# A graph-attention kernel on one core: five row buffers, 64 gathers in the projection block, x loaded inside the attention stage

## The chip, the cores and the metric

The kernel runs on one core of one Trainium2 chip, as one program that does two layers of a graph network with their feed-forward parts. The metric is the device time of one execution in microseconds (us). Engines are named as in the profile: PE (TensorE), DVE (VectorE), ACT (ScalarE), POOL (GpSimd) and SP (SyncE); "POOLq" or "SPq" is an engine's queue of DMA issues.

## The reference, cut to what matters

There are 6250 nodes with 256 features and 100000 edges, sorted by their target `dst`. The first layer is attention over the edges with 8 heads of 32, the second a mean over the same edges. Each is followed by experts.

```python
# layer 0, on x normed by row: W_fc, W_e, attn_* and bias are weights
ft = (feat @ W_fc).reshape(N, H, D)
eh, et = einsum('nhd,hd->nh', ft, attn_h), einsum('nhd,hd->nh', ft, attn_t)
ee = einsum('ehd,hd->eh', (edge_attr @ W_e).reshape(-1, H, D), attn_e)
e = leaky_relu(eh[src] + ee + et[dst])
a = exp(e - segment_max(e, dst)[dst]) / segment_sum(exp(...), dst)[dst]
x = x + segment_sum(ft[src] * a[:, :, None], dst) + bias
x = x + shared(norm(x)) + top-2-of-4 experts(norm(x))
# layer 1: mean over incoming edges of (norm(x) @ W_src)[src], plus the features; batch norm; relu
x = x + that
x = x + expert(argmax(router(norm(x))))(norm(x))       # 32 experts
```

## The kernel before

The 100000 edges are cut into 784 tiles of 128 edges (`ES = 784`), and attend works on chunks of 16 tiles (`UT = 16`), 49 of them (`NCH`). A tile's source rows (256 features and 8 score parts, `RW` = 264 values) are fetched by one indirect DMA on POOL, one index for each of the 128 partitions: `indirect_dma_start(..., SRCT[:, t:t + 1])`. The stages follow each other, each an `nc.Block()` whose end is a barrier of all engines:

- `front` (the projection block) loads x, norms it, multiplies by W_fc and stores the rows `ft_rows` to memory. Beside this it loads `edge_attr` in 49 "edge chunks": SP loads one (L406, L407) when ACT is through with the one before (`attr_T1`), PE transposes it, ACT copies it out (L622), PE multiplies (L531), ACT keeps the result in V (L628). POOL scatters `et` to the edges' starts (L501, 50 indirect DMAs) and then gathers the first two attention chunks, `GF = 2`, 32 tiles (L509). DVE scans F (L835), adds V and F in two halves (L840), and SP stores the halves as `score_parts` (L486).
- `attend` has two blocks. The first (L905 to L950) sets constants: POOL's selection masks and an iota, DVE's memsets and MSEL, which is made of the iota. The second runs the chunks. POOL gathers the rows of chunk c into row buffer c % GS, with `GS = 4`: buffers 0 to 2 lie in `GX`, buffer 3 has its own tile. From chunk 4 on it waits ahead of each four tiles (`WB = 4`) for `g_free`, which PE raises (L1143, L1144) after having waited for its own product of the four tiles. POOL clears the accumulator ACC (L977) after the gathers of chunks 2 and 3, and ACT waits for that before its first instruction. For each chunk SP loads PRE (L1006), DVE makes scores (L1160), running maxima (U_f, L1181), sums and shares in a chain with PE and ACT, multiplies the rows by their weights, four tiles at a time (L1278), and builds the one-hot matrices AHOT (three buffers, L1172); PE multiplies rows by one-hots, tile by tile (L1138), into four PSUM banks, and ACT adds them up in ACC (L1066). The chain of chunk c + 1 is interleaved by hand with the weights of chunk c, in the body `rest`; `first` does chunk 0's chain. The loop is fully written out. When all gathers are out, POOL clears FFN tiles, and SP then loads the FFN weights (L1013).
- `rank_rows` turns ACC and stores it by rows, 49 stores of 128 KB, with 7 row buffers (L1516). In the first layer ("a") SP's queue holds ahead of these the load of the bias and of x (6.4 MB, into `GX`, L1505 and L1508). In the second layer ("b") it has a weight to multiply by and no such loads.
- `gated_experts` uses x and bias. `sum_segments` sums the second layer's rows: 784 gathers (L1376), groups of 8 tiles, 4 groups of buffers, two sets of four PSUM banks; PE waits for each bank (`pfree`) at every second tile. `rank_rows` b, the mean layer and the routed experts follow.

All instructions of an engine run in program order, and DMAs of SP's queue are issued in order.

## Time and profile before

| | |
|---|---|
| median of 3 runs | 4067.09 us (4066.4 to 4073.57) |
| the profiled execution, its own time | 4042.07 us |
| its span in the trace | 4040.4 us |
| mean granted TensorE clock | 0.705 of 2.4 GHz |
| busy over the span | PE 61%, PEld 53%, DVE 50%, POOL 45%, ACT 32% |
| instructions | 51661 |

The stages in the profiled execution, by the starts of their first instructions in the trace: projection block 0 to 485.6 us, attend to 1760.8, rank_rows a to 1825.6, gated experts and norm to about 2340, sum_segments to about 3479, rank_rows b to about 3526, and the rest to 4040.4. The rows further down are read with start and duration in us, then engine, line, operation, output and inputs; the bracket at a row's end is how long the engine had been idle and what released it. "remote" is an event without a recorded sender, "issue" is time in which the engine waited for nothing that the profile shows.

### The profile page before, as it was taken

What the parts mean: (1) busy time and instruction counts of PE and PEld (TensorE: products, weight loads), DVE (VectorE), ACT (ScalarE), POOL (GpSimd) and SP (SyncE); (2) the same over time, 40 slices, a digit from 0 to 9 for tenths busy, and PEclk for the clock granted to TensorE, in tenths of its full rate; (3) what the DMA queues carried; (4) which work ended last, traced back from release to release, by engine and by line L of the source; (5) the groups of instructions that cost most, each with busy time, mean ns of one, the idle gap of its engine ahead of it and who ended that gap; (6) DMA issues with size and microseconds to landing.
All of it is one profiled execution on the core that took longest, in us unless ns stands there. A gap on an engine that the chain in (4) does not pass through costs nothing. (4 is left out here: it accounts for less than half of the span.)

```text
span 4040.4 us, 51661 instructions
## 1 busy us (share of the span) xinstructions
PE 2474.9 (61%) x12916; PEld 2128.5 (53%) x12916; DVE 2006.0 (50%) x6407; ACT 1290.8 (32%) x4654; POOL 1799.1 (45%) x1888
## 2 busy tenths in 40 slices
PE   6964636666666666655899944545545445646348
PEld 5853525555555555544677634544444444535347
DVE  7930247777777777745645432322323223354325
ACT  2311123334334344442233222323323223352113
POOL 0043156666666666403100066666666666241255
PEclk9966666667766776767888856666666666756579
DMA  6343323333333333345000033333333333330043
GB/s 182 100 102 85 120 70 91 91 91 90 89 89 91 91 91 90 76 116 164 20 21 21 18 90 92 90 93 90 93 93 90 93 90 92 103 94 1 25 127 94
DMA packets 262938, 348.49 MB, mean 86 GB/s; under 512 B 153465, under 2 KB 193519, under 8 KB 261143
## 3 DMA queue, kind: packets, MB, share of 16 engines
q0 software_dynamic: 87936, 235.05, 20.8%
q1 hardware_dynamic: 174726, 110.32, 10.7%
q8 instruction: 105, 1.72, 0.2%
q14 instruction: 171, 1.40, 0.1%
HBM read 288.25 MB, written 61.20 MB: 86 GB/s over the span
## 5 line engine op out<-in xcount | busy, mean ns | idle before, releaser
L1376 POOL DMA_INDIRECT Gb<-normed_rows,SRCT x784 | 743.3, 948 | 741.4 <-SPq L1368 358.7
L1396 PE MATMUL pAb<-HOTb,Gb 128*128 128x128 f32 x3136 | 580.5, 336 | 564.0 <-issue 551.2
L1396 PEld LDWEIGHTS pAb<-HOTb,Gb 128*128 128x128 f32 x3136 | 524.2, 247 | 620.6 <-issue 603.5
L1438 DVE TENSOR_TENSOR ACC<-ACC,pAb 128x256 f32 x784 | 330.7, 422 | 800.1 <-DMA sums_by_rank<-rrowa 576.4
L981 POOL DMA_INDIRECT GX<-ft_rows,SRCT x560 | 532.2, 950 | 355.5 <-PEq L1144 211.7
L1138 PE MATMUL apA<-AHOT,GX 128*128 128x129 f32 x2368 | 481.8, 385 | 220.0 <-DVE GX L1278 195.6
L1138 PEld LDWEIGHTS apA<-AHOT,GX 128*128 128x128 f32 x2368 | 449.9, 292 | 255.7 <-DVE GX L1278 223.6
L1066 ACT ACTIVATE ACC<-apA 128x254 f32 x784 | 301.0, 384 | 694.6 <-PE apA L1138 299.1
L1415 ACT ACTIVATE HOTb<-OFFb 128x1024 f32<-128x1024 f32 x98 | 103.6, 1057 | 769.8 <-DMA sums_by_rank<-rrowa 757.5
L1411 ACT ACTIVATE OFFb<-iota,NRELb 128x128 f32<-128x128 f32 x784 | 239.8, 388 | 6.7
L981 POOL DMA_INDIRECT G<-ft_rows,SRCT x192 | 183.2, 954 | 111.0 <-PEq L1144 62.2
L1138 PE MATMUL apA<-AHOT,G 128*128 128x129 f32 x768 | 156.2, 385 | 69.3 <-DVE G L1278 62.9
L1138 PEld LDWEIGHTS apA<-AHOT,G 128*128 128x128 f32 x768 | 145.9, 291 | 80.6 <-DVE G L1278 74.2
L531 PE MATMUL pS<-VB,eT 128*128 128x16 f32 x784 | 117.9, 294 | 109.3 <-issue 60.2
L531 PEld LDWEIGHTS pS<-VB,eT 128*128 128x128 f32 x784 | 113.7, 231 | 124.7 <-issue 62.4
L1278 DVE TENSOR_TENSOR GX<-GX,apV 128x1024 f32<-128x1024 f32 x148 | 176.4, 1193 | 0.4 <-PE apV L1118 0.4
L1605 POOL DMA_INDIRECT Y<-sums_by_rank,RANKI x50 | 48.4, 968 | 241.3 <-POOLq L150 143.0
L1181 DVE TENSOR_TENSOR_SCAN U_f<-PENU,pU 128x128 f32<-128x128 f32 x49 | 20.6, 421 | 243.6 <-remote 194.0
L1067 ACT ACTIVATE FL<-apA 128x4 f32<-128x4 f32 x784 | 134.4, 171 | 0.0
L622 ACT ACTIVATE eT<-pE 128x512 f32<-128x512 f32 x98 | 55.7, 607 | 198.4 <-remote 101.4
L1172 DVE TENSOR_TENSOR AHOT<-apL,RELT 128x1024 f32<-128x1024 f32 x98 | 118.7, 1212 | 0.0
L2180 POOL DMA_INDIRECT rows_by_expert<-PAY,POSI x50 | 49.7, 995 | 150.8 <-DVE POSI L2319 135.9
(386 smaller groups left out, 4615.9 us busy)
## 6 DMA issues: line engine op xcount, KB each, us to landing
ebuf<-in_edge_attr_dram SPq DMA_DIRECT2D x49, 448.0 KB
Gb<-normed_rows,SRCT POOLq DMA_INDIRECT x784
rows_by_expert<-ffn_PADT SPq DMA_DIRECT2D x1, 10360.0 KB
sT<-rows_by_expert SPq DMA_DIRECT2D x80, 129.5 KB
GX<-ft_rows,SRCT POOLq DMA_INDIRECT x592
sums_by_rank<-rrowa SPq DMA_DIRECT2D x49, 128.0 KB, 1.7
sums_by_rank<-rrowb SPq DMA_DIRECT2D x49, 128.0 KB, 1.7
GX<-in_x_dram SPq DMA_DIRECT2D x11, 560.0 KB
```

The costliest lines, as they stand in the source:

```text
L531: last = nc.tensor.matmul(pS[:, m * 2 * H0:(m + 1) * 2 * H0], eT[c % 2][:, m * EP:(m + 1) * EP], VB[:, :], start=True, stop=True)
L981: pool.indirect_dma_start(G[c % GS][:, m, :], None, FT[:, :], bass.IndirectOffsetOnAxis(ap=SRCT[:, t:t + 1], axis=0)).then_inc(g_in[c % GS ...
L1066: nc.scalar.activation(acc[:, :, ds(r + 1, EP - 1)], sums[:, :, 1:EP], ACT.Copy)
L1067: nc.scalar.activation(FL[:, :, f:n + 1:n - f], sums[:, :, 0:HW:EP], ACT.Copy).then_inc(pfree[b], 1)
L1138: last = nc.tensor.matmul(pA[b][:, f * HW:(f + 1) * HW], G[c % GS][:, m, f * 128:(f + 1) * 128], HOT[k][:, m, :], start=True, stop=True)
L1172: nc.vector.tensor_tensor(HOT[k][:, h * HT:(h + 1) * HT, 0:EP], pL[0:EP, 256:256 + EP].unsqueeze(1).to_broadcast([EP, HT, EP]), RELT[:, ds ...
L1278: nc.vector.tensor_tensor(v, v, pV[0:EP, 0:128].rearrange("p (h m) -> p h m", m=UT)[:, :, m:m + WB].rearrange("p h m -> p m h").unsqueeze( ...
L1376: pool.indirect_dma_start(G[g % R][m][:, :], None, TABLE[:, :], bass.IndirectOffsetOnAxis(ap=SRCT[:, t:t + 1], axis=0)).then_inc(g_in[g % ...
L1396: last = nc.tensor.matmul(pA[b][:, o:o + EP], G[k][m][:, c * 128:(c + 1) * 128], HOT[k % 2][:, m, :], start=True, stop=True)
L1411: nc.scalar.activation(OFF[k2][:, m, :], iota[0:EP, 0:EP], ACT.Abs, bias=NREL[k2][:, m:m + 1])
L1415: nc.scalar.activation(HOT[k2][:, :, :], OFF[k2][:, :, :], ACT.Relu, bias=1.0, scale=-1.0).then_inc(hot[k2], 1)
L1438: last = nc.vector.tensor_tensor(acc[:, :, ds(b, EP)], acc[:, :, ds(b, EP)], pA[q][:, o:o + KD * EP].rearrange("p (c r) -> p c r", c=KD), ...
```

## The change

1. `GS` goes from 4 to 5 and `GF` from 2 to 4. The fourth buffer (`G3`) is made before `front`, which now gathers four chunks (64 tiles) at L509's place. To make room, front's scratch tiles share memory, with no additional waits, and AHOT has two buffers instead of three.
2. The add of V and F and the stores of `score_parts` go in seven parts instead of two; part h waits for the first 7 (h + 1) edge chunks instead of all 49.
3. attend's set-up block is merged into the main block. ACT's first instruction waits for DVE's memsets, and ACT waits for ACC at the loading of the first chunk's row numbers, ahead of its first write. POOL clears ACC ahead of its first gather there (chunk 4's), and the FFN tiles between the gathers of chunks 4 and 5. POOL waits for PE's product of the bank directly, and PE does not wait for its own.
4. SP loads bias and x at the end of attend's queue, each part of x behind PE's last product of the chunk whose rows lay there: chunk 45 for the first two parts, 46 and 47 for the others.
5. In `sum_segments` PE waits once in a group of 8 tiles for the last bank of the set, and DVE signals once.

```diff
 SL = 3
-GS = 4
-GF = 2
+GS = 5
+GF = 4
 XPARTS = ((0, 5), (5, 15), (15, 30), (30, NT))
...
+def arow(GX, GE, k, m):
+
+    to, o = (GX, k) if k < SL else (GE, k - SL)
+    return to[:, (o * UT + m) * (D + H0):(o * UT + m + 1) * (D + H0)]
 
...
                     load(c)
                 pv = PRED.rearrange("(p j) h -> p (j h)", j=ES)
-                for h in range(2):
+                for h in range(NPT):
                     a = slice(h * HF * H0, (h + 1) * HF * H0)
                     sp.wait_ge(parts_ready, h + 1)
                     sp.dma_start(pv[:, a], V[:, a]).then_inc(parts_out, 16)
-                sp.wait_ge(parts_out, 32)
+                sp.wait_ge(parts_out, 16 * NPT)
...
                     nc.vector.tensor_tensor_scan(head(h), CONT[:, :], head(h), C0[:, h:h + 1], ALU.mult, ALU.add)
                 dve.drain()
-                dve.wait_ge(v_ready, NCH)
-                for h in range(2):
+                for h in range(NPT):
+                    dve.wait_ge(v_ready, (h + 1) * (NCH // NPT))
                     a = slice(h * HF * H0, (h + 1) * HF * H0)
                     nc.vector.tensor_tensor(V[:, a], V[:, a], F[:, a], ALU.add).then_inc(parts_ready, 1)
...
                     c, m = divmod(t, UT)
+                    if t == GF * UT:
+                        nc.gpsimd.memset(ACC[:, :], 0.0).then_inc(acc_zero, 1)
                     if t == GS * UT:
-                        nc.gpsimd.memset(ACC[:, :], 0.0).then_inc(acc_zero, 1)
...
                     if m % WB == 0 and c >= GS:
 
-                        pool.wait_ge(g_free, c * WG + m // WB + 1)
+                        pool.wait_ge(prod[NBK - 1], (c - GS) * CPB + m // NBK + 1)
                     pool.indirect_dma_start(G[c % GS][:, m, :], None, FT[:, :],
                                             bass.IndirectOffsetOnAxis(ap=SRCT[:, t:t + 1], axis=0)
...
+                xv = x.rearrange("(p i) d -> p (i d)", i=NT)
+                sp.dma_start(BI[:, :], bias.rearrange("h d -> (h d)").partition_broadcast(P)).then_inc(bi_in, 16)
+                for n, (i0, i1) in enumerate(XPARTS):
+
+                    used = max(c for c in range(NCH) if c % GS < SL and c % GS * UT * RW < i1 * D)
+                    sp.wait_ge(prod[NBK - 1], (used + 1) * CPB)
+                    for one in PARTS:
+                        sp.dma_start(X[one, i0 * D:i1 * D], xv[one, i0 * D:i1 * D]).then_inc(xm_in[n], 16)
...
+                    if c == 0:
+                        act.wait_ge(acc_zero, 1)
...
                 act.load(regs[1], BASEI[0:1, 0:HT])
-                act.wait_ge(acc_zero, 1)
+                act.wait_ge(set_ready, 1)
                 unrolled(NCH, SL, first, rest)
                 finish(1, NCH + 1)
...
-                pe.sem_inc(g_free, GS * WG)
-                pe.sem_inc(hot_free, SL)
+                pe.sem_inc(hot_free, 2)
...
                             last = nc.tensor.matmul(pA[b][:, f * HW:(f + 1) * HW], G[c % GS][:, m, f * 128:(f + 1) * 128],
-                                                    HOT[k][:, m, :], start=True, stop=True)
+                                                    HOT[c % 2][:, m, :], start=True, stop=True)
                         last.then_inc(prod[b], 1)
-                        if m % WB == WB - 1:
-
-                            pe.wait_ge(prod[b], c * CPB + m // NBK + 1)
-                            pe.sem_inc(g_free, 1)
                     pe.sem_inc(hot_free, 1)
                     if more:
                         own_shares(c + 1)
...
+                dve.drain()
+                dve.sem_inc(set_ready, 1)
+                nc.vector.tensor_copy(pL[0:EP, 256:256 + EP], iota[0:EP, 0:EP])
...
+                dve.wait_ge(sel2, 1)
+                for h in range(H0):
+                    nc.vector.scalar_tensor_tensor(MSEL[:, :], BU[:, :], float(h * UT), MSEL[:, :], ALU.is_equal, ALU.add)
+                    dve.drain()
+                nc.vector.tensor_copy(pL[:, 400:400 + UT], MSEL[:, :])
+                dve.drain()
...
                         dve.wait_ge(hot_free, c + 1)
-                        nc.vector.tensor_copy(HOT[k][:, :, EP], GOES[:, ds(c * UT, UT)])
-                    nc.vector.tensor_tensor(HOT[k][:, h * HT:(h + 1) * HT, 0:EP],
+                        nc.vector.tensor_copy(HOT[c % 2][:, :, EP], GOES[:, ds(c * UT, UT)])
+                    nc.vector.tensor_tensor(HOT[c % 2][:, h * HT:(h + 1) * HT, 0:EP],
...
                 def group(r, g, k):
                     pe.wait_ge(hot[k % 2], r * 2 + k // 2 + 1)
+
+                    if g >= 2:
+                        pe.wait_ge(pfree[last_bank(k)], r * 2 + k // 2)
                     for m in range(K):
 
                         pe.wait_ge(g_in[k][m], r * 16 + 16)
                         b = bank(k, m)
-                        if m % 2 == 0:
-                            pe.wait_ge(pfree[b], r * 2 + k // 2 + 1)
                         for c in range(KD):
                             o = m % 2 * KD * EP + c * EP
...
-                        if m % 2:
+                        if m == K - 1:
                             last.then_inc(pfree[q], 1)
                         dve.drain()
 
```

On POOL, from the end of front's scatters to the first waits of the loop in the kernel before. GX and G are row buffers, SRCT the indices, arows_free PE's signal, aprod3 the product semaphore of the fourth bank:

```order
L501 DMA et_at_starts<-ETS,FIRSTI 100352x8 x49
L509 DMA GX<-ft_rows,SRCT 128x264 [waits src_ready,row_stored1,row_stored0]
L509 DMA GX<-ft_rows,SRCT 128x264 x31
...
L906 UNCONDITIONAL_BRANCH [waits barrier_Pool_Activation_PE_DVE_SP_gather]
...
L927 IOTA BU 128x16 [waits sel_set]
...
L972 UNCONDITIONAL_BRANCH [waits barrier_Pool_Activation_PE_DVE_SP_gather]
L981 DMA GX<-ft_rows,SRCT 128x264 x16
L981 DMA G<-ft_rows,SRCT 128x264 x16
L977 MEMSET ACC 128x12760
L981 DMA GX<-ft_rows,SRCT 128x264 [waits arows_free]
L981 DMA GX<-ft_rows,SRCT 128x264 x3
```

The same place on POOL in the changed kernel, whose line numbers differ:

```order
L504 DMA et_at_starts<-ETS,FIRSTI 100352x8 x49
L512 DMA GX<-ft_rows,SRCT 128x264 [waits src_ready,row_stored1,row_stored0]
L512 DMA GX<-ft_rows,SRCT 128x264 x47
L512 DMA G<-ft_rows,SRCT 128x264 x16
...
L930 UNCONDITIONAL_BRANCH [waits barrier_Pool_Activation_PE_DVE_SP_gather]
...
L951 IOTA BU 128x16 [waits sel_set]
L957 MEMSET ACC 128x12760
L975 DMA G<-ft_rows,SRCT 128x264 x16
L960 MEMSET ffn_E 128x512
...
L970 AFFINE_SELECT ffn_SEL<-ffn_SEL 4x256 [waits ffn_w_pad]
L975 DMA GX<-ft_rows,SRCT 128x264 [waits aprod3]
L975 DMA GX<-ft_rows,SRCT 128x264 x3
```

The memset of ACC now stands ahead of attend's first gathers, of which 16 are left there instead of 32, and the waits are for the product.

On PE, the second group of four tiles in chunk 0's body and what follows it, in the kernel before (aweighted is DVE's weight multiply, ends_ready its step ahead of the joint maxima):

```order
L1138 MATMUL apA<-AHOT,GX 128x129 [waits aprod3,abank_free0,aweighted]
L1138 MATMUL apA<-AHOT,GX 128x129
...
L1138 MATMUL apA<-AHOT,GX 128x129 [waits abank_free3]
L1138 MATMUL apA<-AHOT,GX 128x129
L1099 MATMUL apQ<-Qends,HSEL 8x112 [waits aprod3,ends_ready]
L1138 MATMUL apA<-AHOT,GX 128x129 [waits abank_free0,aweighted]
```

The same on PE in the changed kernel:

```order
L1130 MATMUL apA<-AHOT,GX 128x129 [waits abank_free0,aweighted]
L1130 MATMUL apA<-AHOT,GX 128x129
...
L1130 MATMUL apA<-AHOT,GX 128x129 [waits abank_free3]
L1130 MATMUL apA<-AHOT,GX 128x129
L1089 MATMUL apQ<-Qends,HSEL 8x112 [waits ends_ready]
L1130 MATMUL apA<-AHOT,GX 128x129 [waits abank_free0,aweighted]
```

The wait for aprod3, PE's own product, is gone ahead of each group and ahead of L1099's step.

On SP, the end of attend's queue and the start of rank_rows', in the kernel before:

```order
L1013 DMA ffn_E<-in_L_ffn_eW_dram 128x64 x4
L971 UNCONDITIONAL_BRANCH [waits ffn_w_in]
L1501 UNCONDITIONAL_BRANCH [waits barrier_Pool_Activation_PE_DVE_SP_release]
L1505 DMA ffn_BI<-in_L_gnn_bias_dram 125x256
L1508 DMA GX<-in_x_dram 112x1280
L1508 DMA GX<-in_x_dram 13x1280
...
L1508 DMA GX<-in_x_dram 112x5120
L1508 DMA GX<-in_x_dram 13x5120
...
L1516 DMA sums_by_rank<-rrowa 128x256
```

The same on SP in the changed kernel:

```order
L993 DMA ffn_E<-in_L_ffn_eW_dram 128x64 x4
L996 DMA ffn_BI<-in_L_gnn_bias_dram 125x256
L1002 DMA GX<-in_x_dram 112x1280 [waits aprod3]
L1002 DMA GX<-in_x_dram 13x1280
...
L1002 DMA GX<-in_x_dram 112x5120 [waits aprod3]
L1002 DMA GX<-in_x_dram 13x5120
L929 UNCONDITIONAL_BRANCH [waits ffn_w_in]
L1506 UNCONDITIONAL_BRANCH [waits barrier_Pool_Activation_PE_DVE_SP_release]
...
L1515 DMA sums_by_rank<-rrowa 128x256
```

The eight loads of x and the bias now stand ahead of the barrier, with waits for PE, and the stores of rank_rows have nothing ahead of them.

## Rows read from the trace of the kernel before

**Rows 1.** Windows: length, busy us of PE, PEld, DVE, ACT, POOL; clock, DMA share.
```profile
311.00:351.00 40.00, 6.96 (x28) 6.19 (x28) 0.00 (x0) 1.36 (x3) 30.30 (x32) 0.54 0.44 118
486.00:557.00 71.00, 1.74 (x6) 0.90 (x6) 14.11 (x66) 2.93 (x7) 43.14 (x41) 0.50 0.29 65
1770.00:1790.00 20.00, 0.00 (x0) 0.00 (x0) 0.00 (x0) 0.31 (x1) 0.00 (x0) 0.59 1.04 231
```

**Rows 2.** L509 as a source line, then POOL's timeline behind it.
```profile
L509 POOL DMA_INDIRECT GX<-ft_rows,SRCT x32: 945/949/999, 310.9 to 349.8; - x32
...
485.62 0.11 POOL L909 MEMSET HSEL<- 128x8 f32 x1 [134.87 <-ACTq L905]
```

**Rows 3.** ACT's timeline beside and behind the gathers: the edge chunks.
```profile
325.64 0.60 ACT L622 ACTIVATE eT<-pE 128x512 f32<-128x512 f32 x1 [10.54 <-remote]
...
362.19 1.09 ACT L622 ACTIVATE eT<-pE 128x512 f32<-128x512 f32 x2 [35.78 <-remote]
...
369.15 0.60 ACT L622 ACTIVATE eT<-pE 128x512 f32<-128x512 f32 x1 [5.70 <-PE pE L522]
```

**Rows 4.** Timeline, end of front and start of attend, DVE and SP.
```profile
472.42 6.76 DVE L840 TENSOR_TENSOR V<-V,F 128x3136 f32<-128x3136 f32 x2 [17.07 <-ACT V L628]
...
488.59 1.68 DVE L945 SCALAR_TENSOR_TENSOR MSEL<-BU,MSEL 128x16 f32<-128x16 f32 x7 [2.49 <-POOL BU L927]
...
491.72 2.73 SPq L1006 DMA_DIRECT2D PRE<-score_parts  x3
...
494.96 0.37 DVE L1160 TENSOR_TENSOR SCT<-GX,PRE 128x128 f32<-128x128 f32 x1 [3.57 <-DMA PRE<-score_parts]
```

**Rows 5.** Timeline, attend's first chain: POOL, ACT and DVE.
```profile
532.14 10.75 POOL L977 MEMSET ACC<- 128x12760 f32 x1
543.02 0.31 ACT L1023 ACTIVATE CTU<-CONTU 128x129 f32<-128x129 bf16 x1 [70.63 <-POOL ACC L977]
...
543.73 0.42 DVE L1181 TENSOR_TENSOR_SCAN U_f<-PENU,pU 128x128 f32<-128x128 f32 x1 [47.99 <-ACT PENU L1024]
...
557.43 1.22 DVE L1278 TENSOR_TENSOR GX<-GX,apV 128x1024 f32<-128x1024 f32 x1
...
560.67 0.38 ACT L1066 ACTIVATE ACC<-apA 128x254 f32 x1 [7.97 <-PE apA L1138]
```

**Rows 6.** Timeline inside the attention loop: POOL and DVE.
```profile
1006.82 0.95 POOL L981 DMA_INDIRECT GX<-ft_rows,SRCT  x1 [0.30 <-issue]
1009.35 0.42 DVE L1181 TENSOR_TENSOR_SCAN U_f<-PENU,pU 128x128 f32<-128x128 f32 x1 [4.28 <-remote]
...
1009.92 0.95 POOL L981 DMA_INDIRECT GX<-ft_rows,SRCT  x1 [2.15 <-PEq L1144]
...
1016.37 0.95 POOL L981 DMA_INDIRECT GX<-ft_rows,SRCT  x1 [1.75 <-PEq L1144]
```

**Rows 7.** Waits from 900 to 1300 us: us in total, times, longest.
```profile
DVE U_f L1181 <- remote: 70.9, 16, 5.3
```

**Rows 8.** DVE's timeline in the last two chunks, without gathers.
```profile
1700.97 0.37 DVE L1160 TENSOR_TENSOR SCT<-G,PRE 128x128 f32<-128x128 f32 x1
...
1703.22 0.42 DVE L1181 TENSOR_TENSOR_SCAN U_f<-PENU,pU 128x128 f32<-128x128 f32 x1 [0.34 <-PE pU L1093]
...
1721.39 0.37 DVE L1160 TENSOR_TENSOR SCT<-GX,PRE 128x128 f32<-128x128 f32 x1
```

**Rows 9.** Timeline of rank_rows a, then SP's stores in rank_rows b.
```profile
1761.12 4.58 SPq L1508 DMA_DIRECT2D GX<-in_x_dram  x8
...
1766.60 56.73 SPq L1516 DMA_DIRECT2D sums_by_rank<-rrowa  x49
...
1796.04 2.49 DVE L1499 COPY rrowa<-pRTa 128x256 f32<-128x256 f32 x7 [27.67 <-DMA sums_by_rank<-rrowa]
...
3482.65 42.74 SPq L1516 DMA_DIRECT2D sums_by_rank<-rrowb  x49
```

**Rows 10.** POOL's timeline in sum_segments, first gather behind a pause.
```profile
2918.01 0.95 POOL L1376 DMA_INDIRECT Gb<-normed_rows,SRCT  x1 [3.26 <-DMA sums_by_rank<-rrowa]
```

More of the change, by code:

```diff
@@ L312, in front @@
         SD = sb(s, "SDa", [P, NT])
[L313 to L314 removed]
         row = [sb(s, f"row{k}", [P, GT, D + H0]) for k in range(2)]
         ETS = sb(s, "ETS", [128, NT * H0])
+        DEG = sb(s, "DEG", [P, NT])
         V = sb(s, "V", [EP, ES * H0])
@@ L843, in attend @@
 def attend(nc, sb, ps, sem, sems, pace, FT, PRED, CONTU, WHOLE, GX, g_in, ident, iota, SRCT, RELT, GOES, BASEI, ACC,
-           FFN, weights):
+           FFN, weights, GE, more):
     NCH = ES // UT
@@ L1120, in first @@
                 def first(c, k, i):
-                    for step in (scores, ends, own_shares, attention, shares_before):
+                    scores(c)
+                    pe.wait_ge(sel2, 1)
+                    for step in (ends, own_shares, attention, shares_before):
                         step(c)
@@ L1421, in _ @@
             def _(dve):
-                for m in range(K):
-                    dve.sem_inc(pfree[m], 1)
                 nc.vector.memset(ACC[:, :], 0.0)
@@ L1444, in _, with rank_rows @@
                 groups(dve, group)
-def rank_rows(nc, sb, ps, sem, sems, pace, tag, ident, weight, ACC, RSUMD, x=None, X=None, xm_in=None, bias=None, BI=None,
-              bi_in=None):
+def rank_rows(nc, sb, ps, sem, sems, pace, tag, ident, weight, ACC, RSUMD):
     K = 7
```

142 lines of the change are left out of this document (63 added, 79 removed).

## The prediction

> **What bounds the kernel now.** I read the busy times by stage first, then the timelines of POOL, ACT, DVE and SP where stages meet, and last the waits inside the attention loop. "B" is the start of attend's first block, 485.6 us here.
>
> Two stretches stand out. From 311 to 351 us DVE does nothing and PE 7 us of 40, while POOL issues 32 gathers; from 486 to 557 us PE is busy for 1.7 us of 71 [rows 1]. In the first, L509's 32 gathers start from 310.9 to 349.8, one every 1.254 us, and end at 350.7 [rows 2]. What the other engines have to do there is the edge chunks (ACT L622 and its like), and ACT gets one of them at 325.64 and the next at 362.19, 11.4 us after POOL's last gather's end; the next comes 7.0 us later [rows 3]. So while POOL issues indirect DMAs, the edge chunks crawl, and that queue, not POOL, sets the end of the projection block: POOL is idle for 134.87 us behind its gathers [rows 2]. I can't name the resource. The row only says "remote".
>
> In the second stretch POOL sets everything: two blocks' set-up, 32 gathers, then the 10.75 us memset of ACC, and behind it ACT's first instruction, which had waited 70.63 us. DVE's U_f waited 47.99 us for it, and the first weight multiply (L1278) starts at 557.43, 71.8 us after B [rows 5].
>
> In the loop a 16-tile chunk takes 25.0 us (16 waits of U_f in 400 us), of which 4.4 us are U_f waiting for "remote" [rows 7]. DVE alone needs 20.4 us: that is the step between two scores (L1160) at the end, where no gather is left to issue and U_f waits 0.34 us [rows 8]. The wait ends 1.6 us after the end of the last gather that POOL could issue (1007.77 to 1009.35), and POOL goes on only 0.6 us later [rows 6]. So the loop is a ring: POOL's burst of eight gathers, release of the others, PE's next four tiles, POOL again.
>
> **The change part by part**, against the profiled execution's 4042.07 us.
>
> (1) 32 more gathers in front: 32 x 1.254 = 40.1 us more stream, 351 to 391 us. In the 36.6 us between ACT's rows at 325.64 and 362.19 one edge chunk got through, so one more will in 40 us. Without the stream a chunk costs 7.0 us at most [rows 3], and I count 4. So I take +36. The bounds are 0 (the chunks run beside the stream) and +40.
>
> The Trainium skill, "DMA: Bandwidth & Descriptors", section "Issuing engines are not separate DMA queues", says that DMAs of all issuing engines run on the same 16 DMA engines and interleave. By that rule the edge loads would share, not stop, and this term would be 0. The rows at 325.64 and 362.19 speak against it, since there the loads' users stand still while the stretch's DMA share is 0.44 [rows 1, 3]; rival A below is this case.
>
> (2) score_parts in seven parts: now the last V is there at 472.4, the two adds behind it take 6.76 us, and the block ends 6.4 us after them [rows 2, 4]. Afterwards only the last seventh is added behind the last chunk, 6.76 / 7 = 1.0 us. That is -5.8; I take -5.5, since the number of stores grows from two to seven, though all but the last lie under the edge chunks.
>
> (3) attend's start. Afterwards no gather and no second barrier stands ahead of the first chain. SP's PRE load needs 3.2 us from issue to scores (491.72 to 494.96, [rows 4]); DVE's eight MSEL steps wait for POOL's iota until B + 3.0 and take 0.24 us each [rows 4], so PRE is there first and scores come near B + 5.3. From scores to U_f is 2 us (1700.97 to 1703.22, with a weight between, [rows 8]), and from U_f to the first weight 13.7 us (543.73 to 557.43, [rows 5]). So the first weight is at B + 21 instead of B + 71.8: -51. The ACC memset runs from B + 2.9 to B + 13.7, under the chain; its first reader's write comes 3.2 us after the first weight (560.67), at B + 24, so it has 10 us to spare and costs nothing, and without that cover it would cost up to 10.75.
>
> (4) Chunk 4's 16 gathers now stand at B + 13.7 to B + 33.8, that is beside chunk 0 and the start of chunk 1, where before POOL had nothing to issue in the first chain. By the ring's rule U_f of chunk 1, due near B + 23, is let go at B + 35.4: +12. In the loop the same wait is 4.4. Bounds 0 and +15; I take +10.
>
> (5) In the loop, POOL waits for PE's product semaphore itself, and PE no longer waits for its own product four times a chunk. POOL's pause is 2.15 us at the burst's end [rows 6] of which the hand-over is a small part, and PE's scores and BU transposes no longer queue behind a completion. I take 0.15 us a chunk, 48 x 0.15 = -7; bounds 0 and -20. A fifth buffer moves which chunk a gather is for, not when its four tiles are done: the release is the product of the current chunk either way. AHOT with two buffers instead of three: DVE writes the one-hots of chunk c + 1 while PE works on c, and the buffer it takes was chunk c - 1's. The wait is met, 0.
>
> (6) The last gathers go out one chunk earlier, so one more chunk has no 4.4 us wait: -4.4. The FFN memsets go ahead of chunk 5's gathers and under the same DVE chain: 0. They are six small steps, once, next to ACC's 10.75 us.
>
> (7) x. Now SP issues the eight x loads at 1761.12, ahead of rank_rows' stores, which share its queue. DVE has copied seven rows and then waits 27.67 us for a store to leave, until 1796.04; all 49 stores take 56.7 us [rows 9]. Without the loads there is no such wait. From 1796.04 on, the 42 stores left need 27.3 us, 0.65 us each; 49 such are 32, and they start some 4 us sooner, without SP's 4.58 us of load issues. So 56.7 + 4 - 32 = 29 less; I take -27. The upper side is 42.7 us for 49 stores, as in rank_rows b [rows 9], which would make it -18; with nothing for the earlier start it is -14. The loads themselves (6.4 MB) now wait for the products of chunks 45 to 47. Ahead of them in SP's queue stand only the PRE and FFN loads, behind them nothing that attend needs, and the last chunks have no other DMA: 0, unless DVE suffers from them (rival D).
>
> (8) sum_segments: PE's waits on banks go from four in a group of eight tiles to one, and DVE's signals too. POOL pauses 3.26 us behind every 16 gathers and everybody starts again with it [rows 10]; that law has no bank in it. 0; bounds +5 and -147 (the pause, 3 us x 49, gone).
>
> Sum: 36 - 5.5 - 51 + 10 - 7 - 4.4 - 27 = **-49**: 3993 us for an execution like the profiled one. The median of the runs is 4067.09, 25 us more, spread over the same work; I keep the difference and not the ratio: 4067 - 49 = **4018 us**.
>
> **Rivals.**
> A. The edge chunks run beside the longer stream. For it: an idle DMA share of over half. Against: rows 3. Then (1) is 0: 4018 - 36 = 3982.
> B. The ring opens, because PE's self-wait was what tied POOL's burst to the others, and sum_segments' law too. For it: the waits end with PE's, every time. Against: POOL, not PE, ends first. 45 chunks x 4.4 = -198, and up to -147 more: 3820 and below.
> C. Slower. PE signals sooner, so the next four tiles are done before POOL's burst of eight ends, and it becomes one of twelve; U_f is then let go four gathers later, 4 x 1.254 = 5.0 us a chunk. For it: POOL needs only 20.1 us of the 25 for its 16 gathers, and it now has a buffer more. Against: the releases inside a chunk are 6.45 us apart (1009.92 to 1016.37, [rows 6]), longer than four gathers take. In all 45 chunks it is +226: 4244; it decides from 49 / 5.0, that is from 10 chunks of 45, and wherever it holds in 12 or more the kernel is slower.
> D. The x loads hold up the last chunks as they held up the stores. Against: what waited there was a store in the same queue. 6.4 MB at the 231 GB/s of that stretch [rows 1] are 27 us of transfer, which would take back all of (7): 4018 + 27 = 4045, still faster.
> E. The change does not do what it says, in that the first chain is held until chunk 4's gathers are out (B + 35.4 plus what is left of the chain, some 15 us): (3) shrinks to -22 and (4) goes: 4037.
>
> **How the numbers follow.** Forecast 0.48; A 0.16; B in full or part 0.10; C 0.11; D 0.09; E 0.06. A difference under 0.2% (8 us) can't be told from no change here, so "same" is 4059 to 4075. The forecast's own bounds: for the fast side (1) part hidden and (5) -20, for the slow side (4) +15 and (7) -14: 3985 to 4040. A, D and E are in 3960 to 4060. The range 3945 to 4072 leaves out B's full form and C: 0.18. Faster: 0.44 of the forecast, all of A and B, 0.05 of D, 0.03 of E: 0.78. Same: 0.04 of the forecast, 0.02 each of C, D and E: 0.10. Slower: 0.09 of C, 0.02 of D, 0.01 of E: 0.12.
>
> **What would show it.** (1) ACT's first edge chunk behind the stream near 402 us instead of 362, the block's end near 516; if near 480, A. (2) One add of 1 us behind the last V. (3) First weight 21 us after the block's start. (4) U_f of chunk 1 with a wait of 10 us or so. (5) U_f still waits some 4 us a chunk on "remote" and POOL still pauses; if these are gone, B; if bursts are twelve long, C. (7) 49 stores in 32 to 43 us and no wait of DVE over 1 us. I am wrong most easily in (1), (4) and the loop, where an unnamed resource is priced by its pattern.

## The result, and the profile after

| | before | changed |
|---|---|---|
| median, 4 runs each | 4070.33 us (4066.4 to 4082.15) | 4009.84 us (4003.71 to 4013.74) |
| ratio | | 0.9843, 95% interval 0.9825 to 0.9862 |
| the profiled execution's span | 4040.4 us | 4012.0 us |

The change takes 60.5 us off, 1.6%; the forecast was 49 off the 4067 known then, at 4018. Measured again on two chips, called chip 1 and chip 14 here, with the kernel before beside it, it gave 0.9855 (0.9838 to 0.9872) and 0.9839 (0.9810 to 0.9867). The two traces differ by 28.4 us only. The profiled execution of before lies 28 us under this median (25 under the 4067), that of the changed kernel 4 us over its own, so terms that are read from this pair of traces do not add up to the measured difference.

Stage by stage in the two traces, with the gap to before that has piled up by then:

| reached | before, us | changed, us | gap |
|---|---|---|---|
| end of the projection block | 485.6 | 521.9 | +36.3 |
| first weight multiply | 557.4 | 545.6 | -11.8 |
| scores of the last chunk | 1721.4 | 1718.6 | -2.8 |
| end of rank_rows a | 1825.6 | 1793.6 | -31.9 |
| end of rank_rows b | 3527.7 | 3494.1 | -33.5 |
| end | 4040.4 | 4012.0 | -28.4 |

Busy times by stage of the changed kernel (window, length, busy us of PE, PEld, DVE, ACT, POOL; clock, DMA share, GB/s), the answer to [rows 1]:

```profile
311.00:351.00 40.00, 6.83 (x28) 6.17 (x28) 0.00 (x0) 1.36 (x3) 30.30 (x32) 0.54 0.44 118
351.00:391.00 40.00, 0.00 (x0) 0.00 (x0) 0.00 (x0) 0.00 (x0) 30.34 (x32) 0.50 0.41 108
486.00:557.00 71.00, 39.84 (x177) 33.28 (x175) 45.07 (x101) 10.37 (x25) 29.78 (x32) 0.57 0.34 90
1770.00:1790.00 20.00, 13.96 (x47) 6.55 (x46) 12.36 (x30) 7.12 (x18) 0.00 (x0) 0.51 0.58 203
```

The first row is as before. The second is the 40 us more of POOL's stream: nobody else does anything. From 486 to 557 PE now works 40 us instead of 1.7, and from 1770 to 1790 the engines work where all stood still.

The gathers of L512 (L509 before) as source lines, with duration in ns and the first and last start:

```profile
L512 POOL DMA_INDIRECT GX<-ft_rows,SRCT x48: 945/949/999, 310.9 to 369.9; - x48
L512 POOL DMA_INDIRECT G<-ft_rows,SRCT x16: 945/949/954, 371.1 to 389.9; - x16
```

ACT's timeline in the changed kernel, beside and behind this stream, the answer to [rows 3]:

```profile
326.07 0.60 ACT L625 ACTIVATE eT<-pE 128x512 f32<-128x512 f32 x1 [10.54 <-issue]
...
393.33 0.60 ACT L625 ACTIVATE eT<-pE 128x512 f32<-128x512 f32 x1 [66.50 <-remote]
402.37 0.60 ACT L625 ACTIVATE eT<-pE 128x512 f32<-128x512 f32 x1 [8.44 <-remote]
402.87 0.27 ACT L631 ACTIVATE V<-pS 128x128 f32<-128x128 f32 x1
```

The same chunk's last row in the kernel before:

```profile
363.16 0.28 ACT L628 ACTIVATE V<-pS 128x128 f32<-128x128 f32 x1
```

An edge chunk is copied in two halves; the row at 362.19 in the kernel before had both, here they come at 393.33 and 402.37. The V row behind them is 39.7 us later (402.87 instead of 363.16), which is 32 gathers. None got through in the longer stream. In both kernels the chunk comes some 11.5 us after the stream's end, not at once.

The timeline from the end of the projection block to chunk 2's scores, the answer to [rows 4, 5]. L843 is the add, L986 the PRE load, L957 ACC's memset, L1167 the scores, L1285 the weight multiply, L1188 U_f:

```profile
517.19 1.09 DVE L843 TENSOR_TENSOR V<-V,F 128x896 f32<-128x896 f32 x1 [10.59 <-ACT V L631]
...
521.95 6.34 SPq L986 DMA_DIRECT2D PRE<-score_parts  x4
...
524.71 10.73 POOL L957 MEMSET ACC<- 128x12760 f32 x1
...
527.50 0.38 DVE L1167 TENSOR_TENSOR SCT<-GX,PRE 128x128 f32<-128x128 f32 x1
```

```profile
530.56 4.92 DVE L1178 COPY AHOT<-GOES 128x16 f32<-128x16 f32 x1
530.62 4.86 DVE L1179 TENSOR_TENSOR AHOT<-apL,RELT 128x1024 f32<-128x1024 f32 x1
531.75 3.73 DVE L1201 TENSOR_TENSOR_SCAN U_fs<-CTU,U_ex 128x128 f32<-128x128 f32 x1
...
535.59 0.23 DVE L1208 TENSOR_SCALAR Qends<-apL,U_f 128x16 f32<-128x16 f32 x1
...
544.89 0.37 DVE L1167 TENSOR_TENSOR SCT<-GX,PRE 128x128 f32<-128x128 f32 x1
...
545.58 1.21 DVE L1285 TENSOR_TENSOR GX<-GX,apV 128x1024 f32<-128x1024 f32 x1
547.76 0.42 DVE L1188 TENSOR_TENSOR_SCAN U_f<-PENU,pU 128x128 f32<-128x128 f32 x1 [0.96 <-PE pU L1083]
...
574.44 0.37 DVE L1167 TENSOR_TENSOR SCT<-GX,PRE 128x128 f32<-128x128 f32 x1
```

Behind the last V one add of 1.09 us is left, and the next stage begins 4.7 us after the add's start, where it was 13.2. Scores come 5.6 us after the block's start and the first weight 23.7. In between stand DVE rows that are new: the copy of L1178 takes 4.92 us (0.15 before), and the rows that start behind it, the one-hots' L1179 and the scan L1201, 4.86 and 3.73 (1.22 and 0.41 before). All three end at 535.48, when POOL's memset of ACC ends (524.71 + 10.73 = 535.44), and the next step follows at once. From L1179's start to L1208's it is 5.0 us where before's trace has 1.9, so the chain loses 3.0 us.

The loop, one burst's end and the release of U_f (answer to [rows 6]), and rank_rows a (answer to [rows 9]), in the changed kernel's timeline:

```profile
1007.50 0.95 POOL L975 DMA_INDIRECT GX<-ft_rows,SRCT  x1 [0.30 <-issue]
1010.23 0.42 DVE L1188 TENSOR_TENSOR_SCAN U_f<-PENU,pU 128x128 f32<-128x128 f32 x1 [3.48 <-remote]
...
1010.88 0.95 POOL L975 DMA_INDIRECT G<-ft_rows,SRCT  x1 [2.44 <-PE apA L1130]
```

```profile
1760.16 31.25 SPq L1515 DMA_DIRECT2D sums_by_rank<-rrowa  x49
1793.64 0.39 SPq L1613 DMA_DIRECT2D rows_by_expert<-ffn_PADT  x1
```

U_f is let go 1.8 us after the end of the last gather of a burst of eight, and POOL goes on 0.65 us later: the ring is as it was. The 49 stores take 31.3 us instead of 56.7.

### The profile page after: what moved, and what is told of

The parts are those of the page before. It is cut to its first block and busy times, and to the rows that moved or that the text cites. A ratio compares the mean times of both kernels' runs of the same rounds, so it can differ in the third digit from the quotient of the medians.

```text
span 4012.0 us, 51163 instructions
## 1 busy us (share of the span) xinstructions
PE 2464.4 (61%) x12916; PEld 2133.0 (53%) x12916; DVE 2006.2 (50%) x6412; ACT 1289.1 (32%) x4654; POOL 1800.5 (45%) x1888
## 5 line engine op out<-in xcount | busy, mean ns | idle before, releaser
L975 POOL DMA_INDIRECT GX<-ft_rows,SRCT x432 | 412.0, 954 | 262.9 <-PE apA L1130 127.5
L1130 PE MATMUL apA<-AHOT,GX 128*128 128x129 f32 x1920 | 396.0, 391 | 171.1 <-DVE GX L1285 146.7
L1130 PEld LDWEIGHTS apA<-AHOT,GX 128*128 128x128 f32 x1920 | 373.0, 298 | 197.0 <-DVE GX L1285 167.2
L975 POOL DMA_INDIRECT G<-ft_rows,SRCT x288 | 274.5, 953 | 172.9 <-PE apA L1130 88.2
L1130 PE MATMUL apA<-AHOT,G 128*128 128x129 f32 x1216 | 244.7, 384 | 101.0 <-DVE G L1285 85.5
L1130 PEld LDWEIGHTS apA<-AHOT,G 128*128 128x128 f32 x1216 | 230.7, 291 | 116.8 <-DVE G L1285 96.5
L1285 DVE TENSOR_TENSOR GX<-GX,apV 128x1024 f32<-128x1024 f32 x120 | 143.1, 1193 | 0.0
L1179 DVE TENSOR_TENSOR AHOT<-apL,RELT 128x1024 f32<-128x1024 f32 x98 | 122.4, 1249 | 0.0
L2379 POOL DMA_INDIRECT out_dram<-sO,sID x80 | 77.8, 973 | 77.7 <-issue 40.9
```

The lines of the kernel that those rows point to most:

```text
L975: pool.indirect_dma_start(G[c % GS][:, m, :], None, FT[:, :], bass.IndirectOffsetOnAxis(ap=SRCT[:, t:t + 1], axis=0)).then_inc(g_in[c % GS ...
L1130: last = nc.tensor.matmul(pA[b][:, f * HW:(f + 1) * HW], G[c % GS][:, m, f * 128:(f + 1) * 128], HOT[c % 2][:, m, :], start=True, stop=True)
L1179: nc.vector.tensor_tensor(HOT[c % 2][:, h * HT:(h + 1) * HT, 0:EP], pL[0:EP, 256:256 + EP].unsqueeze(1).to_broadcast([EP, HT, EP]), RELT[: ...
L1285: nc.vector.tensor_tensor(v, v, pV[0:EP, 0:128].rearrange("p (h m) -> p h m", m=UT)[:, :, m:m + WB].rearrange("p h m -> p m h").unsqueeze( ...
```

## The experiments

Each kernel is the changed one with a short edit. The theory to be tested was the prediction's, called S: a stream of POOL's indirect DMAs starves the other engines, wherever it stands. "To starve" means here that they start next to no instructions. The first four kernels and the kernel before beside them ran on one chip, chip 15.

**Where the gathers stand.** The edit is `GF = 2`.

> The changed kernel with GF = 2: 32 gathers in the projection block instead of 64, and 48 instead of 16 ahead of the first wait in attend (60 us of issue instead of 20). Theory S (a stream of indirect DMAs holds up the other engines wherever it stands): the projection block ends near 482 us instead of 522, and chunks 0 to 3 of attend take about 40 us more, so the total stays within 10 us of the changed kernel's, ratio to before 0.984 give or take 0.002. Rival (the stream costs only in the projection block, since attend's first chain has its rows already and runs beside it): 36 to 40 us less than the changed kernel, ratio near 0.975.

Measured: 4025.53 us, ratio 0.9866 (0.9838 to 0.9895). That is 0.002 above the changed kernel's 0.9843, just outside the 0.002 that were allowed, but its interval covers them. Its timeline, POOL at the block's end and DVE's scores of chunks 1 and 2:

```profile
483.81 0.10 POOL L933 MEMSET HSEL<- 128x8 f32 x1 [131.94 <-POOLq L151]
```

```profile
506.79 0.37 DVE L1167 TENSOR_TENSOR SCT<-GX,PRE 128x128 f32<-128x128 f32 x1
...
583.37 0.37 DVE L1167 TENSOR_TENSOR SCT<-GX,PRE 128x128 f32<-128x128 f32 x1
```

The projection block ends 38.1 us sooner (35 against two kernels on the same chip whose block is the changed kernel's, 518.9 and 519.5), and the step from chunk 1's scores to chunk 2's takes 76.6 us instead of 29.6, 47 more. It is no wait for chunk 2's rows: POOL's 16 gathers for it are out at 517.2. So the 32 gathers cost some 40 us in front or beside the chain, and a little more in attend. The rival, that they cost only in front, falls.

**Cutting the stream in front.** POOL waits for one more edge chunk ahead of every fifth DMA:

```diff
                 for i in range(NT):
+                    if i >= 10 and (i - 10) % 5 == 0:
+                        pool.wait_ge(v_ready, 28 + (i - 10) // 5)
...
                 for t in range(GF * UT):
+                    i = NT + t
+                    if (i - 10) % 5 == 0:
+                        pool.wait_ge(v_ready, min(28 + (i - 10) // 5, NCH))
```

> The changed kernel with POOL's stream in the projection block cut: from its tenth indirect DMA on (50 scatters, then 64 gathers), POOL waits ahead of every fifth for one more edge chunk to be through. Nothing is left out. Theory S with a threshold (the others are held up only once a stream is long, some 10 DMAs or more): edge chunks come every 6 to 8 us from 260 us on, the last V is there near 430 us instead of 517, POOL's last gather near 430 instead of 391, and the block ends 60 to 90 us sooner; total near 3930, ratio near 0.965. Rival N (no threshold: edge chunks and POOL's issue exclude each other at any length): each group of five costs its 6.3 us plus 1.6 us plus a chunk's 5 us, so the 21 chunks end no sooner than now and the block ends at 520 to 560; ratio 0.984 to 0.994.

Measured: 3930.06 us, ratio 0.9636 (0.9607 to 0.9665). It was repeated beside the changed kernel, on chip 14:

> Groups of five indirect DMAs per edge chunk in the projection block, otherwise the changed kernel. On a chip where a chunk takes 25 us: the block ends 80 to 90 us sooner than in the changed kernel of the same call, total 80 us less, ratio 0.964 as before. On a chip where it takes 20: the groups cost 0 to 20 us, since POOL would have finished at 390 and the edge chunks at 400, ratio 0.976 to 0.981.

> The changed kernel beside the kernel before and beside the kernel with groups of five. On a chip where an attention chunk takes 25 us: ratio 0.984 to 0.986 as twice so far, projection block's end near 522 us. On a chip where it takes 20: no starving, the 32 more gathers are hidden, ratio near 0.976, block's end near 404.

Measured: 3902.19 us with groups of five, ratio 0.9633 (0.9607 to 0.9658), and 3988.58 for the changed kernel, 0.9839: 86 us between the two on one chip. POOL's timeline with groups of five on chip 15, at three groups of scatters and at the end of the block:

```profile
270.71 0.97 POOL L506 DMA_INDIRECT et_at_starts<-ETS,FIRSTI  x1 [4.04 <-ACT V L636]
...
277.72 0.97 POOL L506 DMA_INDIRECT et_at_starts<-ETS,FIRSTI  x1 [0.94 <-issue]
...
289.35 0.97 POOL L506 DMA_INDIRECT et_at_starts<-ETS,FIRSTI  x1 [5.55 <-ACT V L636]
```

```profile
434.70 0.10 POOL L938 MEMSET HSEL<- 128x8 f32 x1 [6.29 <-POOLq L151]
```

POOL waits 4.04 us and 5.55 between groups for "ACT V", that is for an edge chunk (0.94 in a third case, put down to "issue"), and idles 6.29 us at the end instead of 131. The block ends at 434.7 us instead of 521.9 (519 on this chip). So the same 114 DMAs and the same 21 edge chunks fit beside each other in this version, and a rule without a threshold (rival N), by which they exclude each other at any length, falls. This version beats both kernels.

But the waits did not cut the whole stream. From 375 to 418.8 us the edge chunks were ahead of them and POOL issued 30 gathers with no pause. Here is what the engines did meanwhile: a window, and rows of DVE, POOL and ACT:

```profile
375.00:390.00 15.00, 14.81 (x60) 12.86 (x60) 13.82 (x8) 2.73 (x6) 12.52 (x9) 0.51 0.65 178
```

```profile
376.18 14.05 DVE L843 TENSOR_TENSOR_SCAN F<-xnT,C,F 128x784 f32<-128x784 f32 x8 [47.43 <-DMA F<-et_at_starts]
380.83 1.44 POOL L517 DMA_INDIRECT GX<-ft_rows,SRCT  x1 [0.30 <-issue]
422.19 1.08 ACT L630 ACTIVATE eT<-pE 128x512 f32<-128x512 f32 x2 [16.23 <-remote]
```

Beside DVE's scans a gather takes 1.44 us instead of 0.95, so that one goes out every 1.74 us and not every 1.25, and PE is busy for 14.8 us of 15, with edge chunks 5 to 7 us apart. Some 9 us after the gathers are back at 1.25 us apart (from 396.5) ACT stops for 16.2 us. The trace from chip 14 has the same: ACT goes on through the gathers of 1.44 us and stops for 8.4 us some 8 us after the full rate is back. So it is not the length alone that starves, but a length at the full rate, and part of this version's gain may come from the slower gathers.

**Longer bursts in the loop.** One wait per chunk:

```diff
-                    if m % WB == 0 and c >= GS:
-                        pool.wait_ge(prod[NBK - 1], (c - GS) * CPB + m // NBK + 1)
+                    if m == 0 and c >= GS:
+                        pool.wait_ge(prod[NBK - 1], (c - GS + 1) * CPB)
```

> The changed kernel with one wait of POOL per chunk in attend, for all 16 tiles of the chunk five before, instead of four waits for four tiles each: bursts of 16 gathers. Theory S: the others are held until the burst is out, U_f's wait goes from 4 us to 8 or more per chunk, a chunk from 25 us to 29 or more, total 150 us or more above the changed kernel, ratio 1.02 or more. Rival P (the pauses at the four waits are what costs, one pause of 3 us takes the place of 2.2 + 1.8 + 1.8): a chunk takes 23 us as 16 gathers do in sum_segments, total 80 to 90 us below the changed kernel, ratio near 0.963.

Measured: 4275.98 us, ratio 1.0484 (1.0455 to 1.0514). DVE's scores of two chunks and POOL's first gather of a burst:

```profile
1004.53 0.37 DVE L1167 TENSOR_TENSOR SCT<-GX,PRE 128x128 f32<-128x128 f32 x1
...
1035.44 0.37 DVE L1167 TENSOR_TENSOR SCT<-GX,PRE 128x128 f32<-128x128 f32 x1
```

```profile
1033.45 0.99 POOL L975 DMA_INDIRECT GX<-ft_rows,SRCT  x1 [11.41 <-PE apA L1130]
```

A chunk takes 30.9 us: some 20 of issue, then POOL idle for 11.4 until PE's last product. The others catch up only in the pause. S said 29 or more, and rival P (23 us) falls. S had also named U_f as the place, and there it was wrong: U_f's wait is 0.3 us or less on average, and DVE waits at the next step, for the exponentials.

**x in the rows' queue.** The loads of bias and x go back to the head of rank_rows.

> The changed kernel with the loads of bias and x back at the head of rank_rows' queue. If the x term stands as the two traces read it (104.2 us from the last scores to the end of rank_rows before, 75.1 after), the total rises by 29 us over the changed kernel, ratio near 0.991. Rival (the loads only moved their cost into the last chunks, and the 29 us come from the end of attend): under 10 us, ratio near 0.985.

Measured: 4041.75 us, ratio 0.9916 (0.9886 to 0.9946), 0.007 above the changed kernel. SP's timeline of it:

```profile
1753.13 4.57 SPq L1505 DMA_DIRECT2D GX<-in_x_dram  x8
1758.60 56.41 SPq L1513 DMA_DIRECT2D sums_by_rank<-rrowa  x49
```

The stores take 56.4 us again, and from the last chunk's scores to the end of rank_rows it takes 101.7 us, where the changed kernel takes 75.1. So the loads cost nothing in the last chunks: the x term stands.

**Four kernels that ran on chip 9.** There the kernel before took 3580.96 us (3574.04 to 3587.09).

> The changed kernel with the projection block's indirect DMAs in groups of ten per edge chunk. Theory S with a threshold of some 10: each group of ten lets one or two edge chunks through, POOL's last gather comes near 410 us, and 11 edge chunks are left for then: the block ends near 470 to 480, total 3965. With a threshold well under ten: as the changed kernel without groups, 10 chunks x 5.3 behind 104 x 1.254 + 10 x 7 us of groups, block end at 500 to 520, total 4000 or more.

> The changed kernel with the projection block's indirect DMAs in groups of three per edge chunk instead of the five of an earlier run, and attend's memset of ACC in eight pieces. Theory S: the edge chunks run at their own 5 to 7 us, the last V comes at 385 to 400 us instead of 427, but 21 chunks let only 63 DMAs through, so 41 gathers follow behind them and POOL ends 51 us later, at 440 to 455; the block ends some 15 us later than with groups of five. Pieces of ACC: if DVE's 4.9 us copy at the start of attend (now 530.6 to 535.5, ending with POOL's memset) is held by that one memset, it takes 1.5 us at most, and the first weight multiply comes 20 us after the block's start instead of 23.7; if not, it stays at 23.7. Total near 3940.

> The changed kernel with two edits in separate stages. In attend POOL waits twice per chunk instead of four times: for eight tiles of the chunk five before, and for the landing of its own last gather, so that bursts are of eight with a pause. In sum_segments POOL waits for the landing of its last gather ahead of every twelfth. Theory S with a threshold of 8 to 10 gathers: an attend chunk takes 16 x 1.254 + 2 x 1.7 = 23.5 us instead of 25.0 (stage 60 to 70 us shorter), and 16 tiles of sum_segments take 20.06 + 4/3 x 1.7 = 22.3 us instead of 23.05 (stage 35 us shorter); total 100 us below the changed kernel, ratio near 0.96. Rival I (what the others need is idle time of POOL, 5 us in 25, however it is cut): a chunk stays at 25 us and sum_segments at 23, ratio near 0.984.

> The changed kernel with two edits in separate stages. In attend POOL waits ahead of every second tile for the product of two tiles (eight waits per chunk). In sum_segments POOL waits for the landing of its last gather ahead of every eighth. Theory S: bursts in attend get shorter and U_f's wait of 3.7 us falls below 2, a chunk takes 23 to 24 us unless the additional pauses, 1.7 us each, make POOL the bound, which would be up to 20.06 + 8 x 1.7 = 33.7 us; sum_segments takes 20.06 + 2 x 1.7 = 23.5 us per 16 tiles, 0.4 more than now (stage 20 us longer). Rival I: both stages unchanged.

The edits, besides the group's length: ACC's memset in eight pieces; a wait at `m % 8 == 0` for eight tiles and for the landing of the gather before; a wait at `m % 2 == 0` for two tiles; and in sum_segments `if t % 12 == 0` (or 8) a wait for the landing of the gather before. Measured, as ratios to before: groups of ten 0.9752 (0.973 to 0.9775), groups of three 0.9903 (0.988 to 0.9926), loop of eight with twelve in sum_segments 1.0608 (1.0587 to 1.063), loop of two with eight 1.0359 (1.0323 to 1.0394). None of the expectations fits, since they were made for a chip that starves. In the kernel with waits for two tiles, whose projection block is the changed kernel's, the busy times of the block's stream and of the loop read:

```profile
311.00:391.00 80.00, 76.29 (x384) 64.92 (x382) 29.69 (x30) 18.56 (x42) 61.72 (x61) 0.67 0.79 237
900.00:1300.00 400.00, 287.08 (x1560) 263.20 (x1560) 352.50 (x1279) 198.24 (x1037) 303.46 (x318) 0.75 0.46 112
```

Beside an unbroken stream PE works 76 us of 80 (7 in the changed kernel's first two rows), and the block ends at 404.2 us. A chunk takes 20.1 us there (20.2 in the kernel with groups of ten, whose loop is the changed kernel's). That is 16 gathers at 1.254 us with no pause of POOL, and near DVE's own time, so it does not say which of the two is the limit. On this chip nothing starves, and rival A's picture of the projection block holds. What is left to read: the extra waits for a landing take 2.3 to 2.5 us each instead of an issue gap of 0.3 (from the end of rank_rows a to the start of b it takes 123 us more with 65 of them than in the kernel with groups of ten, and 220 more with 97), groups of three make POOL the last by 52 us (block end at 456.9), and groups of ten cost nothing (404.5). The unedited changed kernel did not run on this chip. Its time there would be near 3495 us, since the groups of ten change no stage's length; that is a conclusion, not a measurement.

The pieces of ACC answered their question on this chip too. POOL's and DVE's timeline:

```profile
459.73 11.00 POOL L963 MEMSET ACC<- 128x1595 f32 x8
```

```profile
465.64 5.13 DVE L1186 TENSOR_TENSOR AHOT<-apL,RELT 128x1024 f32<-128x1024 f32 x1
```

The DVE step takes 5.13 us, and it ends at 470.77 with the memsets (459.73 + 11.00 = 470.73). So DVE is held through all eight pieces, and not only until the one that is running ends, and the expected 1.5 us is refuted.

**Back on a chip that starves, chip 1.**

> The changed kernel once more, beside the kernel before. The last four kernels ran on another chip than the four ahead of them: there the kernel before took 3581 us instead of 4078, an attention chunk 20.1 us instead of 25.2, and U_f waited under 1 us. If this run falls on such a chip: no starving, so the 32 more gathers in front are hidden (rival A of the prediction), attend's start gives 48, x 29, the seven parts 8, the last chunk nothing: 80 to 90 us of 3581, ratio near 0.976. If it falls on a chip like the first: 0.984 again.

> The changed kernel with three edits in separate stages: groups of ten per edge chunk in front, eight waits per chunk instead of four in attend, and in sum_segments a wait for the landing of POOL's last gather ahead of every twelfth. On a chip where a chunk takes 20 us: front and attend as in the changed kernel, sum_segments 65 x 1.9 = 123 us longer, ratio 1.01. On a chip where it takes 25: front ends at 440 to 480 instead of 522; attend between 20.1 and 25 us a chunk if the length of a burst counts and 25 or more if only POOL's idle time does; sum_segments 35 us shorter by theory S, 60 us or more longer if the pauses only add; ratio 0.95 by S, 0.985 to 1.01 otherwise.

Measured: 3993.97 us, ratio 0.9855 (0.9838 to 0.9872), and 3976.71, 0.9813 (0.9796 to 0.9829). The three edits in their stages, against the changed kernel on the same chip: groups of ten end the block at 479.5 instead of 525.5 us, 46 less; waits for two tiles make a chunk 25.6 us instead of 24.9; waits for the landing at every twelfth gather leave sum_segments as it was (from the end of rank_rows a to the start of b 1639.8 us and 1638.8). In the kernel with all three, DVE's waits from 900 to 1300 us, and POOL's timeline:

```profile
DVE BU L1277 <- remote: 52.8, 14, 4.7
DVE U_f L1193 <- PE pU L1088: 18.4, 15, 1.7
```

```profile
973.80 0.94 POOL L980 DMA_INDIRECT G<-ft_rows,SRCT  x1 [4.68 <-PE apA L1135]
...
985.51 0.94 POOL L980 DMA_INDIRECT G<-ft_rows,SRCT  x1 [2.01 <-remote]
```

U_f's wait for "remote" (71.2 us in the changed kernel on the same chip) is gone, and what is left is 18.4 us for PE. But it has only moved: a later step, BU, now waits 52.8 us for "remote", where it had 5.9. The chunk is no shorter. The edit did not cut the bursts: between 950 and 1100 us POOL's pauses stand in front of every eighth gather, where the changed kernel has bursts of 8, 4 and 4. Nor did it change their sum: without "issue", POOL waits 91.1 us from 900 to 1300 us here and 89.8 in the changed kernel, that is 5.6 to 5.8 us a chunk. So in the loop the theory of a burst's length was not tested downwards (upwards, burst16 did it), and the runs fit rival I, by which the others need some 5 us of POOL's silence in 25, however it is cut; a loop with bursts of four throughout was not tried. They also fit a reading by rate: over a cycle it is one gather per 1.56 us in the loop (25.0 / 16) and one per 1.45 in sum_segments (23.2 / 16), and the 1.74 in the version with groups of five, with no more silence than 0.3 us a gather, starved nobody. That stretch speaks against rival I in its words; no run tests the rate by itself. In front a pause was free, since POOL had 131 us to spare; here POOL has none.

What starving looks like is best seen in sum_segments of the changed kernel, in three windows of one cycle of 16 gathers:

```profile
2892.00:2902.00 10.00, 2.14 (x6) 1.62 (x6) 0.84 (x2) 0.00 (x0) 7.40 (x8) 0.57 0.37 105
2906.00:2912.00 6.00, 6.00 (x37) 6.00 (x37) 3.64 (x9) 5.37 (x17) 4.62 (x5) 0.63 0.38 106
2914.00:2924.00 10.00, 2.07 (x9) 1.83 (x10) 0.84 (x2) 0.00 (x0) 7.56 (x9) 0.66 0.36 107
```

```profile
2898.85 0.37 PE L1404 MATMUL pAb<-HOTb,Gb 128*128 128x128 f32 x1 [1.04 <-issue]
2900.25 0.57 PE L1404 MATMUL pAb<-HOTb,Gb 128*128 128x128 f32 x1 [1.03 <-issue]
...
2904.46 8.77 PE L1404 MATMUL pAb<-HOTb,Gb 128*128 128x128 f32 x51 [0.35 <-issue]
```

POOL issues in all three windows. In the second, just behind its pause, PE runs at full rate (51 matmuls in 8.77 us); in the other two it starts a matmul every 1.4 to 2.1 us once it creeps, also between two of one tile, of which the second has no semaphore to wait for. ACT does nothing at all there. Neither the DMA share (0.36) nor a semaphore explains it. So I read it as something that all engines need to start an instruction and that runs dry some 10 us into a stream at full rate; what it is, no run here shows. The arrival of instruction blocks by DMA it is not, in this cycle: they have queues of their own in the DMA view, of kind "instruction", and from 2889 to 2914 us, while PE creeps, recovers and runs at full rate, the view has no packet but the gathers':

```profile
q0 software_dynamic: 831, 2.25, 31.4%
```

## Why the prediction was right, and where its terms were not

**The total.** 4018 was forecast, 4009.8 measured, well inside 3945 to 4072, and all three measurements of the changed kernel lie between 57 and 62 us under before. That it came out within 8 us is luck in part. The terms as traced come to -28 where -49 was forecast, and the 32 us between -28 and the measured -60 belong to no term: they come from executions of the kernel before that took 28 us more than its profiled one, and of the changed kernel that took 4 less.

**(1), +36, measured +39.7 and then +44.8,** which is outside the term's own bound of +40. The mechanism was right: the first edge chunk behind the stream was forecast near 402 and is through at 402.87. The step that was off is the chunk that should have slipped through; none did. The last V is 44.8 us later than before (516.9 instead of 472.1), 5.1 of it in the chunks behind the stream; the block ends at 521.9 where 516 was forecast. Rival A's picture is right on chip 9 and wrong on the others. So the Trainium skill, "DMA: Bandwidth & Descriptors", section "Issuing engines are not separate DMA queues", by which DMAs of all issuing engines run on the same 16 DMA engines, does not decide it. By the traces these engines are busy for 0.41 to 0.44 of the stretch beside the stream where the others starve, and for 0.79 where they do not, so it is not their time that runs out.

**(2), -5.5, measured -8.5.** The add's part was right; the last store is a seventh in size, too, and the wait behind it shrank with it.

**(3), -51, measured -48.1.** Scores at 5.6 us instead of 5.3, and 3.0 us for DVE steps held by POOL's memset. The claim that the memset costs nothing under the chain failed there; ACT's first write had its room, as forecast. U_f's scan and the steps up to the copy (528.85 to 530.56) ran beside the same memset at their own length, so it is the copy that was held, and what is behind it with it. The Trainium skill, "SBUF — State Buffer", section "🔬 SBUF: two separate sides", has such a rule: VectorE and GpSimd share a pair of ports, which the one that starts first keeps for its whole instruction, and VectorE wants it in its two-port modes. The trace agrees, with the copy held to 0.04 us behind the memset's end, though no row says in which mode the copy ran; and by the kernel with eight pieces a waiting copy does not get in between back-to-back instructions of POOL.

**(4), +10, measured +9.0 in the first trace and +7.1 in the second, at another place.** Chunk 1's U_f was to be held until 35.4 us after the block's start. It waited 0.96 us and came at 25.9, 12 us into the stream. The cost fell on the chunk behind it: 29.6 us from scores to scores instead of 22.7, then 29.1 instead of 25.5, then 22.8 instead of 24.3. The ring's rule left out that the first 10 us of a stream are free.

**(5) and (6), -7 and -4.4.** Between chunks 4 and 45 a chunk takes 25.1 us in the changed kernel's trace, 24.85 and 24.9 in its two others, and 25.0 before. Nothing of 0.15 us can be told from that spread. The last three steps take 61.9 us instead of 68.5, so the end of the gathers did come one chunk earlier, and gave 6.6. Bursts of twelve (rival C) did not come up and were not run; bursts of sixteen cost 5.9 us a chunk and some 260 us in all, where the rival's working, eight gathers more at 1.254 us, gives 10 a chunk: it overstates.

**(7), -27, measured -29.1,** and the experiment with the loads back gives 0.007 of 4078, 30 us. The reading that DVE's 27.67 us were a wait of the stores behind the x loads, and that the loads would do no such harm in the last chunks (rival D), held. Whether the stores waited for their turn in SP's queue or for the DMA engines, whose share was 1.04 there, no run tells apart: the loads were not tried in another queue.

**(8), 0.** Between the ends of the two rank_rows the gap moves by 1.6 us in the first trace, by 11.0 in that of chip 1 and by 8.3 in that of chip 14. The last stage then gives 5.1 us back in the first trace; it takes 512.7 to 517.9 us in the traces of the starving chips, and the change has nothing in it.

What stays open is where the kernel before, in its usual executions, spends the 28 us that its profiled one did not; there is one trace of it, and its stages that starve may vary as those of the changed kernel do, whose three traces differ by 19 us in all.

## What to carry to other kernels

Before moving gathers to where POOL is idle, look at what the other engines do beside POOL's stream: if they stand still there, the place is not free, whatever the DMA share says. Cut such a stream by waits on the work beside it, in groups that leave POOL its slack (here five DMAs per edge chunk, 86 us), but only where POOL has slack: where nothing starved, groups of three took 49 us more than groups of ten (medians 3544 and 3495). And a large load put ahead of small stores in one queue can cost them its whole transfer, here 29 us.

## What the runs showed of the hardware

The kernel before takes 3581 us on one chip and 4050 to 4078 on others. Nearly all of the difference is in stages with streams of indirect DMAs. The changed kernel's trace on chip 1 and that of its version with groups of ten on chip 9 are 496 us apart: 121 in the projection block, 214 from there to the last chunk's scores (20.2 us a chunk instead of 24.9, no pause of POOL), 150 from the end of rank_rows a to the start of b. All runs on chip 9 stand close together in time, so whether it is the chip or something that held just then is not shown. On the chips that starve, the other engines run on for about 10 us into a stream with one gather per 1.25 us. Then, in sum_segments, PE starts one matmul in 1.4 to 2.1 us until POOL pauses; in the projection block PE, DVE and ACT start nothing at all for 40 us (351 to 391), and the next edge chunk comes only 11.5 us behind the stream. Beside gathers 1.74 us apart they run on. And a short DVE copy that meets a POOL memset waits for its end, 3.0 us here and 3.3 with the memset in eight back-to-back pieces, while scans just ahead of it run on. All 13 traces with the memset at this place show it, on every chip: the copy ends 0.03 to 0.04 us behind the memset.
